# Cross attention of a decoder kernel: the row maxima come from the scores themselves, which wait in SBUF

## The reference, cut to what matters

```
q = rms_norm((x_normed @ Wq.T).reshape(4, 256, 16, 128))
kv_in = concatenate([context, x_normed], axis=1)              # 1857 keys
k = rms_norm((kv_in @ Wk.T).reshape(4, 1857, 4, 128))         # 4 key heads, each serves 4 query heads
v = (kv_in @ Wv.T).reshape(4, 1857, 4, 128)
q, k = rope(q, draft_position_ids), rope(k, full_position_ids)
scores = einsum('bhqd,bhkd->bhqk', q, k) * 128**-0.5
attn = einsum('bhqk,bhkd->bhqd', softmax(scores, axis=-1), v)
x = x + attn.reshape(4, 256, 2048) @ Wo.T
```

## Time and profile before

| | |
|---|---|
| median of 3 runs | 1749.54 us |
| profiled execution, first to last instruction (its span) | 1746.4 us |
| prologue of the cross attention, first projection to first score | 440.5 to 497.3 us |
| groups 0 to 14 | 497.3 to about 1600.7 us |
| last group and the end of the cross attention | to about 1657 us |
| busy in one quiet group of 73.6 us: PE, DVE, ACT, POOL | 73.2, 57.2, 34.1, 56.8 us |

### The profile page before, as it was taken

The page is one execution under the profiler, slowest core; times in us unless marked ns, Lnnn a source line. Parts: engine busy times, 40 slices in busy tenths (PEclk is TensorE's granted clock), DMA queues, the critical chain, the costliest instruction groups (busy, mean ns, idle before and its releaser), DMA issues. The chain is left out here.

```text
span 1746.4 us, 27001 instructions
## 1 busy us (share of the span) xinstructions
PE 1567.7 (90%) x8692; PEld 910.2 (52%) x8692; DVE 1320.0 (76%) x2642; ACT 814.5 (47%) x1975; POOL 1141.2 (65%) x1069
## 2 busy tenths in 40 slices
PE   6597796776779999999999999999999999999987
PEld 5476464533434555554555555455555555554454
DVE  7876577878787888788687777968877787776554
ACT  3363664651445454443545444454544444444352
POOL 2362570132667799787779978777987777866642
PEclk9799898978999999999999999999999999999999
DMA  3000820010100000100000100000000000000010
GB/s 97 1 2 30 284 87 25 1 69 0 51 0 13 1 13 1 51 1 1 1 1 1 39 1 1 1 1 1 1 19 1 1 1 1 1 1 1 1 55 25
DMA packets 28498, 38.54 MB, mean 22 GB/s; under 512 B 4804, under 2 KB 24776, under 8 KB 28360
## 3 DMA queue, kind: packets, MB, share of 16 engines
q1 hardware_dynamic: 28360, 36.82, 6.3%
HBM read 35.76 MB, written 1.05 MB: 21 GB/s over the span
## 5 line engine op out<-in xcount | busy, mean ns | idle before, releaser
L2141 POOL TENSOR_TENSOR stream_acc<-stream_acc,stream_p 128x512 f32<-128x512 f32 x448 | 577.0, 1293 | 180.0 <-ACT stream_p L2029 179.0
L2029 ACT ACTIVATE stream_p<-stream_lowered 128x512 f32<-128x512 f32 (+1 forms) x480 | 302.6, 631 | 588.8 <-DVE stream_lowered L2204 584.1
L1964 PE MATMUL stream_banks<-stream_p,stream_v 128*128 128x512 f32 (+1 forms) x960 | 491.5, 594 | 5.5 <-ACT stream_p L2029 5.5
L2204 DVE TENSOR_TENSOR stream_lowered<-stream_banks,stream_shift_all 128x512 f32<-128x512 f32 (+1 forms) x480 | 329.3, 686 | 123.7 <-PE stream_banks L1951 109.8
L2211 DVE TENSOR_REDUCE stream_tops<-stream_banks 128x1 f32<-128x512 f32 (+1 forms) x512 | 324.7, 636 | 95.9 <-PE stream_banks L1937 93.9
L1964 PEld LDWEIGHTS stream_banks<-stream_p,stream_v 128*128 128x128 f32 (+1 forms) x960 | 182.2, 190 | 76.3 <-ACT stream_p L2029 8.0
L1937 PE MATMUL stream_banks<-stream_k_t_hi,stream_q_t_hi 128*128 128x512 bf16 (+1 forms) x512 | 183.7, 360 | 22.1 <-DVE stream_tops L2211 21.0
L1951 PE MATMUL stream_banks<-stream_q_t_hi,stream_k_t_hi 128*128 128x512 bf16 (+1 forms) x480 | 183.0, 381 | 0.0
L1951 PE MATMUL stream_banks<-stream_q_t_lo,stream_k_t_hi 128*128 128x512 bf16 (+1 forms) x480 | 181.9, 379 | 0.0
L1951 PE MATMUL stream_banks<-stream_q_t_hi,stream_k_t_lo 128*128 128x512 bf16 (+1 forms) x480 | 181.9, 379 | 0.0
L2148 POOL TENSOR_TENSOR stream_by_cos<-stream_by_cos,stream_by_sin 128x256 f32<-128x256 f32 x192 | 133.6, 718 | 34.0 <-DVE stream_by_sin L2237 33.8
(11 more groups left out here) (431 smaller groups left out, 2878.2 us busy)
## 6 DMA issues: line engine op xcount, KB each, us to landing
memory_raw_t<-in_ctx_t SPq DMA_DIRECT2D x4, 1601.0 KB, 8.9
row_ctx_t<-in_ctx_t SPq DMA_DIRECT2D x4, 1601.0 KB, 7.3
memory_raw<-in_ctx SPq DMA_DIRECT2D x4, 1536.0 KB
early_raw<-in_L_xattn_Wq SPq DMA_DIRECT2D x4, 512.0 KB, 3.9
stream_raw_o<-in_L_xattn_Wo SPq DMA_DIRECT2D x4, 512.0 KB, 3.8
moe_raw_up<-in_L_ffn_wi SPq DMA_DIRECT2D x6, 256.0 KB, 4.3
model_x<-in_x SPq DMA_DIRECT2D x1, 1024.0 KB, 5.4
self_sm<-in_L_ffn_w_fc SPq DMA_DIRECT2D x1, 1024.0 KB, 6.8
```

The source lines that it names most:

```text
L1964: nc.tensor.matmul(ps[:, 2 + n, :], v[0:r, g % 2, t, :], p32[0:r, step % 4, :], start=(t == 0), stop=(t == KT - 1)).then_inc(weighed, 1)
L2029: nc.scalar.activation(p32[0:r, step % 4, :], lowered[0:r, step % 3, :], ACT.Exp, scale=SCALE).then_inc(p32_ready, 1)
L2141: nc.gpsimd.tensor_tensor(acc[0:r, g % 2, cols], acc[0:r, g % 2, cols], p32[0:r, step % 4, :], ALU.add).then_inc(acc_ready, 1)
L2204: nc.vector.tensor_tensor(lowered[0:r, step % 3, :], ps[0:r, step % 2, :], shift_all[0:r, g % 2, n * HALF:(n + 1) * HALF], ALU.add).then_i ...
```

## The change

The second products are gone. ACT copies each block of scores out of PSUM into one of 21 tiles in SBUF (`rooms`: 19 of its own, and 2 in `ctx_t`, of which the context now takes only two chunk buffers), and DVE keeps a running maximum over the 15 key tiles. The steps run in 32 passes of 15 (a pass is one half of the queries of a group) in place of 16 groups of 30. After a pass PE transposes the 128x512 maxima, DVE reduces them, and they are turned, negated and spread into bank 7. The subtraction and the exp then run in place in SBUF, 18 slots after the score (LOWER), and the weighing and the accumulation 19 slots after it (WEIGH). The copy waits until the tile used 21 steps before is weighed and accumulated. k_t has one buffer instead of two, the prologue has 32 slots, and the variance step of a unit moves from ACT to DVE.

```diff
-STEPS = HALVES * KT
+PAIR = REP // HALVES
+PASSES = GROUPS * HALVES
+STEPS = KT
+ALL = PASSES * STEPS
-AHEAD = 55
+AHEAD = 27
+LOWER = STEPS + 3
+WEIGH = LOWER + 1
+ROOMS = 21
 def start_of(u):
-    return EVERY * u - AHEAD
+    return EVERY * u - AHEAD - (EVERY if u < UNITS else 0)
 def turn_of(u):
-    return start_of(u) + 2 * EVERY - 1 + (EVERY if u < 7 else int(u == 7))
+    return start_of(u) + 2 * EVERY - 1 + (EVERY if u < UNITS else 0)
...
+TOPS_LATE, FLAT_LATE, SPREAD_LATE = STEPS, STEPS + 1, STEPS + 2
+ATT_LATE = STEPS + WEIGH
+SUM_LATE = ATT_LATE + 1
...
                 def score(step):
...
                     if step >= 2:
-                        pe.wait_ge(lowered_ready, step - 1)
+                        pe.wait_ge(maxed, step - 1)
...
+                def turn_most(h):
+                    pe.wait_ge(maxed, STEPS * (h + 1))
+                    wait_bank6("tops", h)
+                    for c in range(4):
+                        last = nc.tensor.transpose(ps[:, 6, c * P:(c + 1) * P], most[:, c * P:(c + 1) * P], const["ident"][:])
+                    last.then_inc(most_turned, 1)
...
+                def spread(h):
+                    pe.wait_ge(flat_ready, h + 1)
+                    if h >= 1:
+                        pe.wait_ge(lowered, STEPS * h)
+                    for c in range(4):
+                        last = nc.tensor.matmul(ps[:, 7, c * P:(c + 1) * P], own[:, c, :], flat[:], start=True, stop=True)
+                    last.then_inc(spread_ready, 1)
...
                 for slot in SLOTS:
                     if 0 <= slot < ALL:
                         score(slot)
-                    pieces = pieces_in(slot)
-                    if 0 <= slot - BEHIND < ALL:
-                        weigh(slot - BEHIND)
-                    for item in pieces[:1]:
-                        piece(item)
+                    if 0 <= slot - WEIGH < ALL:
+                        weigh(slot - WEIGH)
+                    for h in pass_at(slot, TOPS_LATE):
+                        turn_most(h)
+                    for h in pass_at(slot, FLAT_LATE):
+                        turn_top(h)
+                    for h in pass_at(slot, SPREAD_LATE):
+                        spread(h)
...
+                def copy_scores(step):
+                    h, g, n, t = step_of(step)
+                    r = rows_of(t)
+                    ac.wait_ge(scored, step + 1)
+                    if step >= ROOMS:
+                        ac.wait_ge(weighed, step - ROOMS + 1)
+                        ac.wait_ge(acc_ready, step - ROOMS + 1)
+                    nc.scalar.copy(room(step)[0:r], ps[0:r, step % 2, :]).then_inc(copied, 1)
...
                 for slot in SLOTS:
                     if 0 <= slot < ALL:
-                        exponent(slot)
+                        copy_scores(slot)
+                    if 0 <= slot - LOWER < ALL:
+                        exponent(slot - LOWER)
...
                 for slot in SLOTS:
-                    if 0 <= slot < ALL:
-                        accumulate(slot)
+                    if 0 <= slot - WEIGH < ALL:
+                        accumulate(slot - WEIGH)
...
                 def lower(step):
...
                     if t == 0:
-                        ve.wait_ge(side_taken, side_at[("spread", g, n)] + 1)
-                    ve.wait_ge(scored, step + 1)
-                    if step >= 3:
-                        ve.wait_ge(p32_ready, step - 2)
-                    nc.vector.tensor_tensor(lowered[0:r, step % 3, :], ps[0:r, step % 2, :], shift_all[0:r, g % 2, n * HALF:(n + 1) * HALF],
-                                            ALU.add).then_inc(lowered_ready, 1)
+                        ve.wait_ge(spread_ready, h + 1)
+                    nc.vector.tensor_tensor(room(step)[0:r], room(step)[0:r], ps[0:r, 7, :], ALU.add).then_inc(lowered, 1)
+
+                def keep_most(step):
...
+                    ve.wait_ge(copied, step + 1)
+                    if t == 0:
+                        if h >= 1:
+                            ve.wait_ge(most_turned, h)
+                        nc.vector.tensor_copy(most[:], ps[:, step % 2, :]).then_inc(maxed, 1)
+                    else:
+                        ve.wait_ge(maxed, step)
+                        nc.vector.tensor_tensor(most[0:r], most[0:r], ps[0:r, step % 2, :], ALU.max).then_inc(maxed, 1)
+
+                def take_top(h):
+                    ve.wait_ge(most_turned, h + 1)
...
+                    nc.vector.tensor_reduce(top[:], ps[:, 6, :].rearrange("p (c n) -> p c n", c=4), AX_X, ALU.max).then_inc(top_ready, 1)
...
+                def vary(u):
...
+                    nc.vector.tensor_scalar(var[:, u % 2, 0:n], ss[:, u % 2, 0:n], 1.0 / HD, 1e-6, ALU.mult, ALU.add).then_inc(var_ready, 1)
```

409 lines of the change are left out of this document (184 added, 225 removed).

## The result

| | before | changed |
|---|---|---|
| median of 4 runs each, us | 1749.12 | 1732.64 (1730.69 to 1732.77) |
| ratio | 1 | 0.9895, 95% interval 0.9874 to 0.9917 |
| span of the profiled run, us | 1746.4 | 1730.7 (run 1732.53) |
| mean granted clock | 0.965 | 0.953 |

The change gains 16 us (1%), and the interval of the ratio keeps clear of 1. A gain of 65 us was forecast (1684 us, with a range from 1652 to 1718), so the forecast was too fast by 49. First the shares of the engines, from the page's first part.

What follows compares the result with a forecast made beforehand. PE was taken to bound the kernel; -75 quiet groups, +1.3 last group, -24.4 prologue, +7 fill, +5.5 drain, +8 and +12 row changes sum to -65.6: span 1680.8, plus 3.1, forecast 1684 us, range 1652 to 1718.

Steps and rivals of the forecast that it cites:

- What bounds: Cross attention, quiet groups: PE sets the pace, with 71.4 of 72.6 us of work per group.
- What leaves PE: Quiet group: second score products take 6.3 us away, transposes and a turn add 0.9 and 0.1; net -5.3.
- PE is held 0.1 to 0.3 us per pass end: Pass ends: new waits around transposes and spread cost 0.3 per group, giving -5.0, 67.6 us per group, -75 over 15 periods.
- The closed loop: Score, copy, maximum before a bank is overwritten: 2.2 us against 3.0 for two slots; fits unless ACT or DVE is late.
- DVE: Quiet group: maxima and `vary` come, pieces' reductions go; busy 61.8 of 67.6 us, 91%, `vary` 3.7 of it.
- DVE becomes the bound: Rival, chance 0.12: DVE's unhidden waits set the pace at 70.5 us per group; 1728 us in all.
- The faster rival: Chance 0.13: PE feels no row-change delays, fill at 1.25 per slot, waits ahead of pieces go (-15); -104.6, 1645 us.
- ACT and POOL: Quiet group: ACT gains copies, busy 49 of 67.6 us, hidden; POOL keeps 56.8, 84% of the period.
- the slower rival: Chance 0.04: POOL's additions wait out DVE's operations in SBUF, 75.1 us per group; +86, 1835 us.
- The ends: Prologue: first score at about 460.3, net -24.4; first 19 slots without weighing at 1.45 each, +7.
- The drain: Last 19 slots: PE only weighs while POOL's additions need 1.24 to 1.29 each; +5.5.
- The changes of row: Three places: sines delaying exp cost 2.7 more each (+8), POOL's table writing 4 each (+12).

Runs made afterwards that it cites:

- e1: Changed kernel with `vary` placed behind the maximum in its slot, nothing else changed; 1708.7 us, quiet group 69.3 us.
- e3: Changed kernel with a pass's two output products 8 and 13 slots into the next pass instead of 6 and 9; 1716.3 us, quiet group 69.5.
- e5: Changed kernel with weighing two slots after lowering instead of one, 22 tiles, output products at slots 8 and 13; 1696.9 us, quiet group 68.7.
- e9: Changed kernel with late `vary`, weighing two slots after lowering, 22 tiles, row sums at slot 5, output products at 8 and 10; 1685.6 us.
- e4: Changed kernel with 14 of 15 maxima per pass left out, scores waiting for the copy instead (cost probe); 1704.3 us, quiet group 69.1.

## Why the prediction was wrong, point by point

- **What bounds: right.** PE does, before and after. In the group of 70.5 us no other engine is busy over 57.2.
- **What leaves PE: right.** Net -5.3 was forecast; by the rows' distances the work fell from 71.4 to 66.3, so by 5.1.
- **"PE is held 0.1 to 0.3 us per pass end ... with 0.3 per group": this is the step that failed.** The standing grew by 2.9. The pass ends are near what I said (0.2 to 0.45 each, as the tenths are counted). The term for waits anywhere else in a quiet group stood at nothing, without a reason. I looked for new waits only at the pass ends, where the change adds semaphores, and not where it puts old work in front of new: the even pass, where the change strings rotation, `vary`, maximum and additions to x together. I had even written down "slots 5 to 9: DVE 11.1, PE 11.4" and used it only as a ground for the rival of a full DVE. The 2.9 us by which 70.5 misses the forecast of 67.6, times 14, are 40 of the 50 us missing. e1, e3 and e5 each take away a part of it, and e9, at 67.8, all but 0.2.
- **The closed loop: the wrong loop was worked out.** I computed 2.2 of 3.0 us for score, copy and maximum, "unless ACT or DVE comes late by over 0.8", and PE waited for it only 8.6 us in all. What I left out is the chain of lowering, exp and weighing, with one slot (36.3 in all, 1.27 in the quiet group looked at), and the use of bank 6 behind the additions to x (18.5 in all, 1.24 in that group).
- **DVE: size wrong, harmless.** 61.8 were forecast and 57.2 measured. `vary` had a median of 160 ns instead of over 400: four of six are free. But the two that are not stand in the worst slots; a mean over the group (3.7 forecast, about 3.0 measured) hid that. So `vary` makes up 0.7 of the 4.6. Another part is what goes: the pieces' reductions show 21.1 us of records in a quiet group before (33 of 639 ns), where 17.8 was put (and 24 x 0.6 + 8 x 0.4 is 17.6). The rest stays open.
- **The rival "DVE becomes the bound" gave 70.5 per group, which is the number measured, for a wrong reason.** DVE idles 13.3 of 70.5, and PE waits little for `most`. Taking 16.4 us per group from DVE (e4) gave only 1.4 per group.
- **The faster rival: its counterargument was misread.** Most waits on second products were said to lie in the prologue; of the 22.1 us 7.4 lie ahead of the first score. The waits did go, but new ones of more than that took their place, so this decided nothing.
- **ACT and POOL: right.** POOL 56.2 (56.8 forecast), additions 1296 ns against 1293; the slower rival, DVE's blocks holding up POOL, is out. The blocking that does show goes the other way, POOL holding `vary` on DVE. ACT 45.7 (49).
- **The ends: right at the start.** The first score starts at 460.10 (460.3 forecast) and the first weighing at 489.84; the fill of 19 slots takes 29.7 (27.6), within the 40 that I had set as its limit:

```profile
460.10 0.38 PE L1947 MATMUL stream_banks<-stream_q_t_hi,stream_k_t_hi 128*128 128x512 bf16 x1
...
489.84 1.12 PE L1979 MATMUL stream_banks<-stream_weights,stream_v 128*128 128x512 f32 x2 [1.52 <-ACT stream_weights L2042]
```

- **The drain: mechanism half right.** The weighings did not come 1.25 apart. PE does them in bunches when the exp is there, and then waits once, 4.2, for POOL's last addition. The stretch of the last two groups to the end of the stage is 3.4 longer than before.
- **The changes of row: right.** With the rest of the first group, in which the first of them lies, they cost 18.7 more than before, 20 forecast. At each of the three PE waits up to 4.0 before a weighing; at the second it was 2.2 before, and 4 to 5 were forecast. The waits from 820 to 864 us, around the second:

```profile
PE stream_banks L1979 <- ACT stream_weights L2042: 4.8, 3, 4.0
```

- **The sum.** Of the miss of 50 us, 40 are the quiet groups, 2 the prologue, -1 the changes of row, and 9 the last two groups (one more at 2.9, the drain) with the stage behind them (2.4, below).
